# Routing spread over five slots, two sums and a mixing product a slot later, ScalarE's order of units turned, and the last expert's product in two halves

## The reference

```
x = x + 0.5 * ffn(layernorm(x))      # 8 experts, F = 512, softmax router, top 2
x = x + attn(layernorm(x))
x = x + 0.5 * ffn(layernorm(x))

ffn:  h = relu(x @ w1[e].T + b1[e]);  y[e] = h @ w2[e].T + b2[e]   for all 8 experts
      out = sum over the top 2 of  y[e] * weight[e]
attn: z = tanh((x + delta*mu_x) @ W_x1.T)          # delta = shifted x - x, W_x1 has 160 rows
      five mixes x + delta*(z_i @ W_x2_i + bias_i) -> r, w, k, v, g
      S = exp(-exp(w_t)) * S + k_t v_t^T ;  o_t = r_t (S + u k_t v_t^T)   # scan over 1024 steps
      group norm of o, times silu(g), times W_o
```

## Time and profile before

| | |
|---|---|
| median of 3 runs | 498.45 us (498.34 to 499.76) |
| the profiled execution | 498.35 us, of which 496.3 us from its first to its last instruction |
| granted TensorE clock | 0.999 |
| busy share of the span | PE 97%, DVE 71%, ACT 64%, POOL 46% |
| DMA | 44.57 MB, mean 90 GB/s |

### The profile page before, as it was taken

How to read it: one execution, slowest core, us unless ns; L and a number is a source line. 1 busy time by engine, 2 the same in 40 slices (tenths; PEclk the granted TensorE clock), 3 DMA queues, 4 the chain that set the end, 5 groups by cost and what they waited for, 6 DMA issues and landing times.

```text
span 496.3 us, 6148 instructions
## 1 busy us (share of the span) xinstructions
PE 482.4 (97%) x1833; PEld 296.0 (60%) x1833; DVE 353.3 (71%) x685; ACT 317.8 (64%) x540; POOL 230.2 (46%) x252
## 2 busy tenths in 40 slices
PE   8997999999999999999999989999999999999996
PEld 4675775565546546545744745555566555777774
DVE  3889877759964875995486899934759994567644
ACT  3775786676646667564656765545786555787773
POOL 3234532627865162785416168724625873431322
PEclk9999999999999999999999999999999999999999
DMA  8761120058310017640003554111026621002200
GB/s 257 255 232 44 42 64 23 23 158 224 128 42 1 1 44 209 176 126 1 1 3 127 148 166 149 48 65 42 0 92 182 195 65 42 1 0 115 79 1 21
DMA packets 21296, 44.57 MB, mean 90 GB/s; under 512 B 3856, under 2 KB 4240, under 8 KB 21264
## 3 DMA queue, kind: packets, MB, share of 16 engines
q1 hardware_dynamic: 14928, 32.66, 20.7%
q10 hardware_dynamic: 6336, 11.54, 7.8%
HBM read 40.91 MB, written 3.28 MB: 89 GB/s over the span
## 4 chain that ended last, share of the span: by engine, by line
PE 83%; DVE 7%; issue 5%; ACT 3%; POOL 2%; POOLq 0%; ACTq 0%; DVEq 0%
PE Y L354 24%; PE U L331 11%; PE U L335 10%; PE U L334 10%; PE Y L349 4%; PE Y L350 4%; PE Y L351 4%; PE A L423 3%; PE A L415 2%; PE A L409 1%; PE Y L358 1%; DVE hid_lo L742 1%; PE A L382 1%; ACT xnt L521 1%; PE A L442 1%
## 5 line engine op out<-in xcount | busy, mean ns | idle before, releaser
L549 ACT ACTIVATE hid<-U,small 128x512 f32<-128x512 f32 x161 | 110.4, 689 | 95.5 <-PE U L335 95.1
L354 PE MATMUL Y<-hid,w 128*128 128x512 f32 x322 | 164.2, 591 | 0.0
L331 PE MATMUL U<-xhi,w1lo 128*128 128x512 f32 x256 | 160.4, 626 | 1.1 <-ACT hid_hi L547 0.6
L890 POOL TENSOR_TENSOR xT<-xT,gy 128x512 f32<-128x512 f32 x63 | 82.2, 1304 | 157.8 <-DVE gy L751 157.6
L334 PE MATMUL U<-xlo,w1hi 128*128 128x512 f32 x256 | 100.6, 393 | 0.2 <-DVE xlo L683 0.2
L335 PE MATMUL U<-xhi,w1hi 128*128 128x512 f32 x256 | 100.8, 394 | 0.0
L742 DVE TENSOR_TENSOR hid_lo<-hid,hid_hi 128x512 fp32r<-128x512 f32 x95 | 76.1, 809 | 34.6 <-ACT hid_hi L547 34.2
L546 ACT ACTIVATE hid<-U,small 128x512 f32<-128x512 f32 x95 | 65.5, 689 | 40.1 <-PE U L335 36.5
L331 PEld LDWEIGHTS U<-xhi,w1lo 128*128 128x128 f32 x256 | 48.2, 188 | 62.4 <-issue 52.2
L916 POOL TENSOR_TENSOR qs<-q,pool_a 128x512 f32<-128x512 f32 x64 | 76.0, 1187 | 17.4 <-DVE pool_a L791 17.2
L334 PEld LDWEIGHTS U<-xlo,w1hi 128*128 128x128 f32 x256 | 48.4, 189 | 35.5 <-issue 32.4
(11 more groups left out here) (126 smaller groups left out, 511.5 us busy)
## 6 DMA issues: line engine op xcount, KB each, us to landing
G<-gate_dram SPq DMA_DIRECT2D x32, 512.0 KB, 4.3
vb<-v_dram ACTq DMA_DIRECT2D x44, 256.0 KB, 3.4
vb<-v_dram SPq DMA_DIRECT2D x20, 256.0 KB, 4.4
pool_a<-wexp_dram SPq DMA_DIRECT2D x8, 256.0 KB, 6.7
w<-wexp_dram SPq DMA_DIRECT2D x8, 256.0 KB, 6.7
v_dram<-v SPq DMA_DIRECT2D x8, 256.0 KB, 2.2
xnt<-xtok_dram SPq DMA_DIRECT2D x4, 256.0 KB, 4.8
xT<-xT_dram SPq DMA_DIRECT2D x4, 256.0 KB, 7.3
```

The source lines that it names most:

```text
L331: mm(dst, w1lo[:, e, f, :], xhi[:, k % NB, :], start=True, stop=False)
L354: mm(dst, w2[:, g % E, f, :], hid[:, n % HS, :], start=first, stop=final).then_inc(down, 1)
L549: act.activation(hid[:, n % HS, :], U[n % 2][:, :], ACT.Relu, bias=bias).then_inc(h_f, 1)
L890: pool.tensor_tensor(xT[:, h, b, :], xT[:, h, b, :], gy[:, g % 2, :], ALU.add).then_inc(acc, 1)
```

## The change

Six edits:

1. For blocks 1, 2 and 3 the routing steps 1 to 5 are issued one a slot (t = 8 to 12) where three slots held (1, 2), (3, 4), (5). The gates' way to DRAM is issued two slots later for these blocks. Blocks 0 and 4 to 7 keep three slots.
2. `reduce` 0, 1 and 2 of each unit stand a slot later on PE (t = 25, 30, 35, were 24, 29, 34). The fourth stays at t = 39.
3. Of the product with W_x1, the second one (32 rows, bank A[2]) and its tanh stand a slot later, and so does PE's wait for `x_att` of the unit before, which stood ahead of the first one.
4. ACT goes through the units from the youngest to the oldest in a slot.
5. In both split products the matmul with the low half of the moving operand (`xlo`, `hid_lo`) is the third of its three; it was the second. The wait for `hid_lo` stands ahead of that matmul alone.
6. The last expert's second product is made in two halves of 256 tokens in two banks (Y[1] and A[0]), and `finish` waits for each half.

The diff at its core:

```diff
+REDUCE = (T_SC + 7, T_SC + 12, T_SC + 17, T_SC + 21)
...
+def route_steps(k, t):
+    if not 0 <= t < route_slots(k):
+        return ()
+    return (t + 1,) if route_slots(k) == 5 else ((1, 2), (3, 4), (5,))[t]
+
+def route_slots(k):
+    return 5 if k in (1, 2, 3) else 3
...
-    return max(4 * (k * E + (c + 1) * EQ - GS) + 4, PREP[k] + T_RT + 3 if k else 0)
+    return max(4 * (k * E + (c + 1) * EQ - GS) + 4, PREP[k] + T_RT + route_slots(k) if k else 0)
...
# PE, ffn_up
                 mm(dst, w1lo[:, e, f, :], xhi[:, k % NB, :], start=True, stop=False)
+                mm(dst, w1hi[:, e, f, :], xhi[:, k % NB, :], start=False, stop=False)
                 if f == 0 and e == 0:
                     pe.wait_ge(xn_lo, k + 1)
-                mm(dst, w1hi[:, e, f, :], xlo[:, k % NB, :], start=False, stop=False)
-                mm(dst, w1hi[:, e, f, :], xhi[:, k % NB, :], start=False, stop=True).then_inc(up, 1)
+                mm(dst, w1hi[:, e, f, :], xlo[:, k % NB, :], start=False, stop=True).then_inc(up, 1)
# PE, ffn_down
+                halves = [(Y[g % 2][:, :], slice(0, NT))]
+                if g == BLOCKS * E - 1:
+                    halves = [(Y[g % 2][:, 0:NT // 2], slice(0, NT // 2)), (A[0][:, 0:NT // 2], slice(NT // 2, NT))]
+                pe.wait_ge(h_f, n + 1)
                 if in_parts(n):
...
+                    for dst, cut in halves:
+                        mm(dst, w2lo[:, g % E, f, :], hid_hi[:, at, cut], start=first, stop=False)
+                    for dst, cut in halves:
+                        mm(dst, w2hi[:, g % E, f, :], hid_hi[:, at, cut], start=False, stop=False)
                     pe.wait_ge(h_lo, parts_to(n + 1))
-                    mm(dst, w2lo[:, g % E, f, :], hid_hi[:, at, :], start=first, stop=False)
-                    mm(dst, w2hi[:, g % E, f, :], hid_lo[:, at, :], start=False, stop=False)
-                    mm(dst, w2hi[:, g % E, f, :], hid_hi[:, at, :], start=False, stop=final).then_inc(down, 1)
+                    for dst, cut in halves:
+                        last = mm(dst, w2hi[:, g % E, f, :], hid_lo[:, at, cut], start=False, stop=final)
+                    last.then_inc(down, 1)
# PE, attend
                 if t == T_Z:
...
+                    mm(A[1][:, :], w(W_X1, P), xm, start=True, stop=True).then_inc(z_p, 1)
+                if t == T_Z + 1:
                     if i >= 1:
                         pe.wait_ge(x_att, i)
-                    mm(A[1][:, :], w(W_X1, P), xm, start=True, stop=True).then_inc(z_p, 1)
                     mm(A[2][0:32, :], w(W_X1 + P, 32), xm, start=True, stop=True).then_inc(z_p, 1)
...
-                if T_SC + 6 <= t <= T_SC + SC + 1 and (t - T_SC) % 5 == 1:
-                    reduce(i, (t - T_SC) // 5 - 1)
+                if t in REDUCE:
+                    reduce(i, REDUCE.index(t))
# ACT
-                for i in range(UNITS):
+                for i in reversed(range(UNITS)):
                     attend(i, step_of(i, n))
# DVE, finish
-                dve.wait_ge(down, (g + 1) * FC)
                 dve.wait_ge(acc, g)
                 for c in range(2):
...
+                    bank = (Y[g % 2], A[0])[c][:, 0:NT // 2]
+                    dve.wait_ge(half_y, c + 1)
```

More of the change, by code:

```diff
@@ L342, in ffn_down @@
                     pe.wait_ge(comb, g - 1)
-                dst, first, final = Y[g % 2][:, :], f == 0, f == FC - 1
+                first, final = f == 0, f == FC - 1
+                halves = [(Y[g % 2][:, :], slice(0, NT))]
+                if g == BLOCKS * E - 1:
+                    halves = [(Y[g % 2][:, 0:NT // 2], slice(0, NT // 2)), (A[0][:, 0:NT // 2], slice(NT // 2, NT))]
+                pe.wait_ge(h_f, n + 1)
                 if in_parts(n):
@@ L347, in ffn_down @@
                         pe.wait_ge(w2lo_s, g)
+                    for dst, cut in halves:
+                        mm(dst, w2lo[:, g % E, f, :], hid_hi[:, at, cut], start=first, stop=False)
+                    for dst, cut in halves:
+                        mm(dst, w2hi[:, g % E, f, :], hid_hi[:, at, cut], start=False, stop=False)
                     pe.wait_ge(h_lo, parts_to(n + 1))
-                    mm(dst, w2lo[:, g % E, f, :], hid_hi[:, at, :], start=first, stop=False)
-                    mm(dst, w2hi[:, g % E, f, :], hid_lo[:, at, :], start=False, stop=False)
-                    mm(dst, w2hi[:, g % E, f, :], hid_hi[:, at, :], start=False, stop=final).then_inc(down, 1)
-                else:
-                    pe.wait_ge(h_f, n + 1)
-                    mm(dst, w2[:, g % E, f, :], hid[:, n % HS, :], start=first, stop=final).then_inc(down, 1)
+                    for dst, cut in halves:
+                        last = mm(dst, w2hi[:, g % E, f, :], hid_lo[:, at, cut], start=False, stop=final)
+                    last.then_inc(down, 1)
+                else:
+                    for dst, cut in halves:
+                        last = mm(dst, w2[:, g % E, f, :], hid[:, n % HS, cut], start=first, stop=final)
+                        if len(halves) == 2:
+                            last.then_inc(half_y, 1)
+                    if len(halves) == 1:
+                        last.then_inc(down, 1)
             def keep_clock(n):
@@ L761, in finish @@
                     at = slice(c * NT // 2, (c + 1) * NT // 2)
-                    link(dve.scalar_tensor_tensor(out=gy[:, g % 2, at], in0=Y[g % 2][:, at], scalar=w(W_B2 + g % E, 1),
+                    bank = (Y[g % 2], A[0])[c][:, 0:NT // 2]
+                    dve.wait_ge(half_y, c + 1)
+                    link(dve.scalar_tensor_tensor(out=gy[:, g % 2, at], in0=bank, scalar=w(W_B2 + g % E, 1),
                                                   in1=G[:, g % GS, at], op0=ALU.add, op1=ALU.mult))
@@ L774, in prepare @@
                     route(k, 0)
-                if T_RT <= t < T_RT + 3:
-                    for step in ((1, 2), (3, 4), (5,))[t - T_RT]:
-                        route(k, step)
+                for step in route_steps(k, t - T_RT):
+                    route(k, step)
             def scan(i, m):
@@ L870, in _ @@
                 if 1 <= n < 4:
-                    for step in ((1, 2), (3, 4), (5,))[n - 1]:
+                    for step in route_steps(0, n - 1):
                         route(0, step)
```

4 lines of the change are left out of this document (2 added, 2 removed).

## The result

The changed kernel takes 493.21 us (median of 4 runs, 492.99 to 493.53) beside 499.11 us for the kernel before on the same chip (4 runs, 498.34 to 499.76): ratio 0.9883, 95% interval 0.9862 to 0.9903, so 1.2% faster. The forecast of 494.3 is 1.1 us too high; the range of 492.3 to 496.6 held the time. Two gaps have to be explained. The first: from profiled execution to profiled execution, on which the sum was built, the gain is 4.8 us (498.35 to 493.53) and not 4.05. The second: the medians differ by 5.9, another 1.1 more.

A forecast was written before the change was run, and what follows sets the result against it. TensorE bounds the kernel, busy 482.4 of 496.3 us, so only its 13.9 us of waits can be won. Terms 0.6 + 0.6 − 0.05 + 1.0 + 0.6 + 0.9 + 0.4 = 4.05 from 498.35 give 494.3 us, range 492.3 to 496.6.

The forecast's parts named there:

- Block 1 (0.6): Slot 19's `hid_lo` stall nearly goes, but split weights are late next at slot 24: 0.6 us gained, from 0 to 2.4.
- only its 0.55 of idle time in it: Block 1: DVE's chain to the weights for slot 24 can shorten only by 0.55 us idle, plus what order changes.
- So I take 0.6, not 2.4: Block 1: the gain taken for slot 19's stall, since DVE's chain to slot 24's weights caps it.
- Block 2 (0.6): Slot 44: one routing step less ahead of `xm` removes PE's 0.55 us wait; 0.6 gained, lower bound 0.3.
- Block 3 (0.05): Slot 89: step 5 falls before unit 1's fourth mix, which has 1.5 us slack; cost 0.05, from 0 to 0.6.
- W_x1 (1.0): Slot 128: moving the `x_att` wait to the second product removes the whole 0.94 us wait; 1.0 gained, bounds 0.6 and 1.15.
- a bracket understates what PE loses by up to 0.2: All PE stalls: a matmul's record outlasts its step, so the listed idle time is short by up to 0.2 us.
- Sums (0.6): Unit 2: first sum's 1.34 us wait shrinks, fourth sum gets a new wait of some 0.7; 0.6 gained, 0.3 to 1.3.
- ScalarE's order (0.9): Unit 3: normalising during ACT's wait for POOL removes PE's 0.74 us wait, plus earlier `relu`; 0.9 gained, bounds 0.4 and 1.1.
- counted as nothing: Edit 5, split matmul order: apart from slot 19 it works only at the very start, at most 0.1 us.
- Halves (0.4): Tail: DVE's last four steps and the store start 0.43 us earlier, half matmuls cost nearly nothing; 0.4 gained, lower bound 0.
- Block 1 keeps the whole stall: Rival, chance 0.12: DVE's chain before slot 24 turns out shorter, so block 1 gives 2.4 instead of 0.6; 492.3 us.

The follow-up runs named there:

- after_again: The changed kernel itself, unaltered, timed once more as a control: 493.09 us, ratio 0.9880 to the kernel before.
- u1_fill: Changed kernel with blocks 1 to 3 routed in three slots again, plus two useless FP32 matmuls in slot 19's stall: 494.40 us (495.85 without those matmuls).
- v_route12: Changed kernel with only block 3's routing back in three slots, blocks 1 and 2 still in five: 493.37 us.
- u3_z: Changed kernel with edit 3 undone, both W_x1 products and both tanh in one slot behind the `x_att` wait: 494.51 us.
- u2_reduce: Changed kernel with edit 2 undone, sums 0 to 2 back at t = 24, 29, 34: 493.67 us.
- v_late5: Changed kernel with steps 3 to 5 of block 5's routing moved from slots 138 and 139 to 160 and 161: 492.26 us.
- u4_act: Changed kernel with edit 4 undone, ScalarE going through the units from the oldest again: 494.42 us.

## Why the prediction came out as it did

- **Block 1 (0.6).** Right in mechanism, too small in size, and right in its number by luck. Slot 24 does come 0.60 earlier (49.08 to 48.48), because the weights' subtraction ends at 47.45 + 0.88 = 48.33 instead of 48.93. But this execution came to slot 19 late by 0.42, so the stretch itself gave 1.02 up to slot 24 (1.03 in after_again, whose start was early) and 0.84 up to slot 25. The step that was off is "only its 0.55 of idle time in it": from the arrival of the router's logits on VectorE (`lsum`, 30.34 before, 30.89 after) to the end of that subtraction the chain takes 18.59 us before and 17.44 after. Of the 1.15 that is gone, 0.55 is the idle time. Most of the rest is blocked steps, for which the prediction added nothing: summed over that chain, what instructions took beyond the usual length of their kind (0.69, 0.41 and 0.19 us) is some 4.25 us before and 3.75 after. The expected short wait for `w1lo` is there, twice (0.65 at slot 20, 0.20 at slot 24). The port, too: in VectorE's rows after, one tiny step is held by POOL's addition (36.92 to 38.23) and one by the weight split (38.76 to 39.82), as counted; each ends within 0.05 us of POOL's end, as the page "SBUF — State Buffer" of the Trainium skill, section "SBUF: two separate sides", has it.

```profile
36.98 1.30 DVE L741 TENSOR_TENSOR rt<-rt,const 128x32 f32<-128x32 f32 x1
...
39.21 0.66 DVE L748 TENSOR_TENSOR rt<-rt,rs 128x32 f32<-128x32 f32 x1
```

- **What is missing: "So I take 0.6, not 2.4" as the whole price of that stall.** The price left out that a long stall can lower the granted clock behind it. For the changed kernel with the stall put back, this is shown: 1.45 us in the median (u1_fill). For the kernel before it is argued from its runs: in the three groups 16 of 21 had a mean clock of 0.996 to 0.998 and a median of 499.42, the other five 0.999 or 1.000 and a median of 498.67. No profile of a run of the first kind was taken, and a mean of 0.998 can also come from a fall behind PE's last matmul, as in after_again. The execution whose trace was read was one of the undisturbed kind, with the clock at 1.00 in every window of 38 to 50 us. So the second gap: the median of before lay 0.8 above the execution that the sum was made against (499.11 to 498.35), which the clock would account for by its size; the other 0.3 is the changed kernel's own profiled execution, the slowest of its four, with 0.94 of waiting at the start.
- **Block 2 (0.6).** Right: no wait before the `xm` product at 82.52, lead up by 0.61 from slot 25 to 48; in u1_fill, with this block's routing back in three slots, it changes by −0.04 there.
- **Block 3 (0.05).** Too small: it costs 0.3 at slot 92, and PE does wait for the fourth mix, by 0.17, which the prediction had named as a sign of error. A tiny instruction of step 5 (`L757`, 128x4) took 1.05 us there instead of 0.16, until one of POOL's mixes ended (178.01), and the mix behind it began only at 178.66; the range of 0 to 0.6 held it. Its price in the total is nothing (v_route12), because the fourth sum would have taken 0.3 back anyway.

```profile
176.98 1.05 DVE L757 SCALAR_TENSOR_TENSOR rs<-rs 128x4 f32<-128x4 f32 x1
...
178.66 1.37 DVE L834 SCALAR_TENSOR_TENSOR pool_a<-A,small,qs 128x512 f32<-128x512 f32 x2
```

- **W_x1 (1.0).** Mis-sized low: 1.27 by the lead, 1.3 by u3_z, above the upper bound of 1.15. The step that failed is "a bracket understates what PE loses by up to 0.2". The bracket shows 0.94. By the starts, the matmul ahead of the wait begins at 252.46 and needs 0.86 to the next start (251.40 to 252.26 in the changed kernel), so PE stands from 253.32 to 254.43, 1.11; and the product behind the wait then takes 1.02 to the next start (254.43 to 255.45), 0.16 more than the 0.86 of its kind. The bracket was short by 0.33.
- **Sums (0.6).** Right in size and in mechanism: 0.61 by the lead, 0.5 to 0.6 by u2_reduce, the new wait 0.84 where 0.7 was said. v_late5 shows that the cap is VectorE's chain with block 5's routing in it.
- **ScalarE's order (0.9).** 1.13 by the lead, 1.2 by u4_act, just above the bound of 1.1: mechanism right, but the part above the bracket was put down to the earlier `relu`, and the rows of u4_act show it at the wait itself, 0.16 ahead of it and 0.25 behind it. It is the same understated bracket as at W_x1.
- **Edit 5, "counted as nothing".** Wrong. It is worth 0.8 to 1.1 when undone alone. 0.54 of this lies in block 1's stretch; the 0.29 that the lead gains from slot 170 to 185 stands in no term. The earlier trace rows showed `hid_lo` behind VectorE's work at quarters 17 and 18 as well, and only slot 19 was counted.
- **Halves (0.4).** 0.26 to 0.29 in the rows: 0.70 from the last pair to VectorE, not 0.6, and a little lost in the starts at 0.12.

The first gap, term by term: block 1 +0.24 (0.84 of lead for 0.6), W_x1 +0.3, ScalarE +0.2, slot 185 +0.3, time outside the span +0.2, and +0.26 by which the lead creeps up from slot 48 to 89; less the start −0.42, block 3 −0.2 and the halves −0.1. That makes about the 0.75 between 4.8 and 4.05. Of the 0.26, 0.17 comes behind the three moved sums of unit 0 (lead 1.02 at slot 60, 1.19 at slot 80); with edit 2 undone the lead stands at 1.49 at both, so this is edit 2 at a place for which the sum had nothing. The other 0.09 is in u2_reduce and in the other profiled executions too, and is put to no edit. So that the forecast came within 1.1 us is in part luck: a late start of 0.42 in the profiled execution and a cost of block 3 set off part of the gains that were counted too low. The undone edits sum to more than the whole (2.6 + 0.5 + 1.3 + 1.2 + 1.1 + 0.5 = 7.2 against 5.9) for two reasons: the 2.6 holds 1.45 of clock, of which the 5.9 holds 0.8 at most, and edits 1 and 5 work on the same stall (by slot 25 they lose 0.90 and 0.54 when undone alone, where both together gave 0.84). The rival "Block 1 keeps the whole stall" gave 492.3, about as far from the measured time as the forecast, but its mechanism did not happen to its size: up to slot 24 the stretch gave 1.0, not 2.4.

## What to carry to other kernels

For each stall that goes, name what is late next and read its margin there; here this gave 0.6 for a stall of 2.4, which was worth 0.84, and 0.6 for one of 1.3, which held. Read a stall from the starts of the matmuls on both sides of it and not from its bracket: here brackets of 0.94 and 0.74 stood for 1.27 and 1.13. Compare two executions stretch by stretch and take their starts off, or a late start hides a gain. Price a long stall of TensorE twice, once as a wait and once as a risk to the clock behind it, and look at the mean granted clock of every run, not only of the profiled one; where the fall lies, only a profile shows. If such a stall can't be removed, matmuls into an idle bank can be worth more than they cost, as they were here (1.45 us in the median).

## What the runs showed of the hardware

- After PE had been idle for 1.96 and 0.66 us with one matmul between, the granted clock was 0.59 and 0.56 in the rows from 44 to 48 us, and matmuls of 512 columns started 0.43 instead of 0.23 us apart; then it was 1.00 again. The profiled execution of the kernel before, with a stall of 2.36 us at the same place, and another run of the same kernel (494.12 us, mean clock 0.999) did not have it: it is a matter of the single execution.
- A VectorE instruction that reads only 128x4 values was stretched from 0.16 to 1.05 us, and one of 128x32 from 0.19 to 1.30, while POOL ran a tensor operation. In these rows the price of such a meeting was what was left of POOL's operation, not the size of VectorE's own work.
- Split matmuls of 256 columns, each with its own weights of 128 columns, start 0.12 us apart, about half of the 0.23 of 512 columns (eighteen took 2.14 us where nine of twice the columns took 2.05 to 2.08).
- Next to a wait PE loses more than the gap in its records: a plain product of 512 columns behind a wait took 1.02 us to the next start and not 0.86, and the record ahead of the wait is itself 0.16 longer than its step (1.02 against 0.86).
